# A fused attention and experts kernel: another order of the mixed stage, and the first transposition of the maxima moved into the attention

## The reference

```
x = x + attention0(group_norm(x))      # 6 heads of 16; relative position bias over rows and columns; no mask
t = x as tokens (1024, 96)
t = t + attention1(layer_norm(t))      # 6 heads of 16; causal mask
t = t + experts(layer_norm(t))         # 4 experts 96 -> 384 -> 96, softmax gate, the best 2 kept
```

## Time and profile before

| | |
|---|---|
| median of 3 executions | 2171.5 us (2166.65 to 2174.11) |
| the profiled execution | 2174.62 us, its span 2172.8 us, mean granted PE clock 0.929 of full speed |
| PE busy | 1873.2 us, 86% of the span |
| DVE busy | 1246.8 us, 57% |
| ACT busy | 1121.3 us, 52% |
| POOL busy | 145.3 us, 7% |

### The profile page before, as it was taken

One profiled execution on the slowest core, in us unless ns is written; L12 is line 12 of the kernel. 1 busy time (PEld: TensorE's weight loads), 2 busy tenths in 40 slices (PEclk: granted clock), 3 DMA queues, 4 the chain that ended last, 5 costly groups with the idle time before them and its releaser, 6 DMA issues.

```text
span 2172.8 us, 29007 instructions
## 1 busy us (share of the span) xinstructions
PE 1873.2 (86%) x9408; PEld 750.1 (35%) x9408; DVE 1246.8 (57%) x2508; ACT 1121.3 (52%) x1423; POOL 145.3 (7%) x69
## 2 busy tenths in 40 slices
PE   2696589988899888997899978998789988999858
PEld 1132233433334333343333433343333433334323
DVE  6671676456773567545665557645677357753631
ACT  3256245663466544673456734566346654556333
POOL 3000002000020001100020000200002000200000
PEclk7598599998999899999999989999899999999979
DMA  6326300632026300263004530064102630001200
GB/s 142 49 48 98 73 11 18 114 67 41 17 54 99 66 22 18 51 96 66 22 18 91 73 64 11 21 114 73 33 18 53 99 66 13 18 11 41 43 11 8
DMA packets 55742, 111.45 MB, mean 51 GB/s; under 512 B 17687, under 2 KB 18904, under 8 KB 54041
## 3 DMA queue, kind: packets, MB, share of 16 engines
q1 hardware_dynamic: 54040, 109.06, 26.9%
q10 hardware_dynamic: 1536, 0.30, 0.1%
HBM read 61.82 MB, written 34.60 MB: 44 GB/s over the span
## 4 chain that ended last, share of the span: by engine, by line
PE 67%; DVE 15%; issue 6%; ACT 5%; DMA 4%; SPq 1%; POOL 1%; DVEq 0%; ACTq 0%; POOLq 0%
PE psOM L646 15%; PE psS L592 12%; PE psT L621 8%; PE psT L622 7%; DVE mx L1280 6%; PE psT L756 6%; PE psS L770 5%; PE psT L624 3%; DVE mrow L1382 2%; PE psT L542 2%; DVE qb L1409 2%; DVE x L1391 1%; DMA qr<-negb 1%; PE psT L551 1%; PE psOM L567 1%
## 5 line engine op out<-in xcount | busy, mean ns | idle before, releaser
L1007 ACT ACTIVATE probs<-psT 128x1024 f32<-128x1024 f32 (+7 forms) x768 | 622.9, 838 | 540.2 <-PE psT L622 267.7
L1280 DVE TENSOR_REDUCE mx<-psS 128x1 f32<-128x512 f32 (+3 forms) x1152 | 704.4, 644 | 312.1 <-PE psS L592 233.6
L622 PE MATMUL psT<-qb,kb 97*128 97x512 f32 x768 | 417.2, 587 | 0.0
L646 PE MATMUL psOM<-probs,v 128*32 128x512 f32 (+3 forms) x2688 | 385.0, 558 | 13.0 <-ACT probs L1007 13.0
L592 PE MATMUL psS<-ka,qa 128*128 128x512 bf16 x768 | 300.9, 401 | 37.6 <-DVE mx L1280 18.8
L621 PE MATMUL psT<-qa,ka 128*128 128x512 bf16 x768 | 297.6, 388 | 16.4 <-DMA qb<-negr 8.1
L1409 DVE TENSOR_TENSOR qb<-psOM,qa 32x768 fp32r<-32x768 f32 x128 | 121.8, 952 | 139.7 <-ACT qa L1047 137.9
L756 PE MATMUL psT<-xf,w1s 97*128 97x512 f32 x384 | 198.4, 650 | 1.8 <-DVE mrow L1382 1.8
L770 PE MATMUL psS<-probs,w2s 128*96 128x512 f32 x384 | 189.8, 622 | 0.8 <-ACT att L1072 0.8
L624 PE MATMUL psT<-qr,kr 97*128 97x512 bf16 (+3 forms) x576 | 183.9, 346 | 3.5 <-DMA qr<-negb 1.3
L1064 ACT ACTIVATE probs<-psT 128x1024 f32<-128x1024 f32 x96 | 98.4, 1025 | 158.9 <-PE psT L756 158.3
(11 more groups left out here) (146 smaller groups left out, 1651.4 us busy)
## 6 DMA issues: line engine op xcount, KB each, us to landing
scr<-split SPq DMA_DIRECT2D x32, 576.0 KB, 4.5
scr<-qb SPq DMA_DIRECT2D x16, 768.0 KB, 6.6
qr<-scr SPq DMA_DIRECT2D x48, 192.0 KB, 6.8
au<-ot SPq DMA_DIRECT2D x192, 32.0 KB, 2.0
lb<-ot SPq DMA_DIRECT2D x192, 32.0 KB, 2.0
qr<-scr SPq DMA_DIRECT2D x48, 128.0 KB, 4.4
kr<-scr SPq DMA_DIRECT2D x48, 128.0 KB, 7.3
qa<-scr SPq DMA_DIRECT2D x32, 128.0 KB, 3.8
```

The costliest lines, as they stand in the source:

```text
L622: last = mm(o[:, a:b], kb[:, h, ks], qb[:, h, a:b], start=False, stop=True)
L646: last = mm(psO[j:j + 2 * HD, a - c * HALF:HALF], v[:, kt, 2 * p + hh, :], probs[:, (2 * kt + hh) % 4, a:(c + 1) * HALF], start=kt == 0, s ...
L1007: A(probs[:, n % 4, q0:T], psT[:, t_slot(ts, m), q0:T], ACT.Exp).then_inc(t_free, 1)
L1280: V.reduce_max(mx[layer][:, p % 2, (h % 2) * NT + t, kc:kc + 1], psS[:, s_bank(st, fill), 0:max_cols(layer, t, kc)], AX).then_inc(s_free, 1)
```

## The change

(In the first line "before" has H6 L6 behind d7.) The diff, cut to its core:

```diff
-"u11 m7 m8 m9 m10 d10 m11 m12 b2 m13 m14 d11 m15 b3 tmax")
+"u11 m7 m8 m9 m10 d10 m11 m12 b2 m13 m14 d11 m15 b3")
...
             def transpose_max(it, layer, p):
                 ms, n = att_m(layer, p)
-                pe.wait_ge(rowmax, upto("rowmax", it, ms, n + 1))
+                if layer == 1 and p == 0:
+                    pe.wait_ge(t_free, upto("t_free", it, ms, 0))
+                else:
+                    pe.wait_ge(rowmax, upto("rowmax", it, ms, p if layer else n + 1))
...
-                        if layer == 1 and p == 0:
-                            pe.wait_ge(y_free, upto("y_free", it, st, 0))
                         pe.wait_ge(o_free, upto("o_free", it, st, p))
...
                 if layer == 1:
+                    pe.wait_ge(y_free, upto("y_free", it, st, 0))
+                    transpose_max(it, 1, 0)
                     pe.wait_ge(l1_in, upto("l1_in", it, "attn1", 0))
                     for fill in range(LEAD):
                         max_scores(it, st, fill)
...
                     else:
-                        pe.wait_ge(negmax_in, upto("negmax_in", it, st, 16 * p))
+                        pe.wait_ge(negmax_in, upto("negmax_in", it, st, 16 * (p + 1)))
...
-            def first_rows(it, st):
-            def first_negated(it, st):
...
                 if layer == 1:
+                    neg_max(it, 1, 0)
                     exp_table()
```

More of the change, by code:

```diff
@@ L77, in seq @@
             for w in text.split()]
-MIX = seq("gate gates u0 u1 R0 d0 H0 L0 H1 L1 v0 u2 d1 v1 ln den R1 u3 d2 u4 H2 L2 u5 res H3 d3 nrm L3 u6 d4 d5 tr R2 H4 L4 q0 q1 lev V0 d6 V1 "
-          "u7 H5 L5 R3 u8 d7 H6 L6 H7 L7 u9 b0 d8 u10 b1 m0 m1 m2 m3 d9 m4 m5 m6 "
-          "u11 m7 m8 m9 m10 d10 m11 m12 b2 m13 m14 d11 m15 b3 tmax")
+MIX = seq("gate gates u0 u1 R0 d0 H0 L0 H1 L1 v0 u2 d1 v1 ln den R1 u3 H2 L2 d2 H3 u4 res d3 nrm L3 u5 d4 tr u6 R2 H4 L4 d5 q0 q1 V0 lev V1 "
+          "H5 L5 u7 d6 u8 R3 H6 L6 d7 H7 L7 u9 b0 d8 b1 u10 m0 m1 m2 m3 d9 m4 m5 m6 "
+          "u11 m7 m8 m9 m10 d10 m11 m12 b2 m13 m14 d11 m15 b3")
 def there(stage, kind):
@@ L112, in fills @@
 def fills(stage, kind):
-    return [x for x in steps(stage, kind) if x[0] in ("up", "max", "tmax", "res", "tr", "qk", "val", "val0")]
+    return [x for x in steps(stage, kind) if x[0] in ("up", "max", "res", "tr", "qk", "val", "val0")]
 def by_act(what):
-    return what[0] in ("up", "tr", "tmax", "val", "val0")
+    return what[0] in ("up", "tr", "val", "val0")
 _ATT = {"attn0": 1, "attn1": 1}
@@ L136 @@
     "t_full": {"p_qkv0": 4, "attn1": ATT_FILLS, "attn0": QKV_AT, "qkv0": 2,
-               "attn0b": ATT_FILLS - QKV_AT, "rel": 2, "a": NE * HJ, "next_mix": 7 + 2 * NT},
+               "attn0b": ATT_FILLS - QKV_AT, "rel": 2, "a": NE * HJ, "next_mix": 6 + 2 * NT},
     "s_full": {**{s: len(m) for s, m in MAX_STEPS.items()}, "norm": 4, "a": 2 * NE},
-    "m_full": {"attn1": PAIRS - 1, "lead": 1, "attn0": PAIRS - 1, "a": 1},
+    "m_full": {"attn1": PAIRS, "lead": 1, "attn0": PAIRS - 1, "a": 1},
     "gsum_full": _GN, "gsum_free": _GN,
@@ L151 @@
     "rowmax": {"attn1": PAIRS - 1, "lead": 1, "attn0": PAIRS - 1},
-    "negmax_in": {"attn1": 16 * (PAIRS - 1), "lead": 16, "attn0": 16 * (PAIRS - 1), "next_mix": 16},
+    "negmax_in": {"attn1": 16 * PAIRS, "lead": 16, "attn0": 16 * (PAIRS - 1)},
     "p_used": {s: ATT_FILLS for s in _ATT},
@@ L162 @@
     INCS[f"{_r}_free"] = dict(INCS[f"{_r}_full"])
-INCS["ta_free"] = {"p_qkv0": 2, "rel": 2, "a": NE * HJ, "next_mix": 4}
+INCS["ta_free"] = {"p_qkv0": 2, "rel": 2, "a": NE * HJ, "next_mix": 3}
 INCS["r_free"] = {"qkv0": 2}
@@ L217, in att_m @@
 def att_m(layer, p):
-    return ("attn1", p - 1) if layer else ("attn0", p - 1) if p else ("lead", 0)
+    return ("attn1", p) if layer else ("attn0", p - 1) if p else ("lead", 0)
 def next_layer0(it):
@@ L841, in mix @@
                         first_maxima(it, "mix", n)
-                    elif what == "tmax":
-                        first_rows(it, "mix")
-            def first_rows(it, st):
[L847 to L851, removed]
             def group_means(it, st):
@@ L966, in neg_max @@
                 act.wait_ge(m_full, upto("m_full", it, ms, n + 1))
-                act.wait_ge(negmax_in, upto("negmax_in", it, ms, 16 * max(p - 2, 0) if layer else 0))
+                act.wait_ge(negmax_in, upto("negmax_in", it, ms, 16 * max(p - 1, 0) if layer else 0))
                 A(negm[layer][:, p % 2, :], psM[0:2 * NT, 0:P], ACT.Copy, scale=-1.0).then_inc(m_free, 1)
@@ L1083, in mix @@
                         rel_high(it, "mix", n)
-                    elif what == "tmax":
-                        first_negated(it, "mix")
                     elif what == "up":
@@ L1283, in maxima @@
                         dve.wait_ge(s_free, upto("s_free", it, st, fill + 1))
-                        dve.wait_ge(m_full, upto("m_full", it, st, max(p - 1 - layer, 0)))
+                        dve.wait_ge(m_full, upto("m_full", it, st, max(p - 1, 0)))
                         V.tensor_tensor(mrow[:, p % 2, :], mx[layer][:, p % 2, :, 0], mx[layer][:, p % 2, :, 1],
```

## The result

The changed kernel has a median of 2159.99 us over 10 runs (2150.72 to 2170.08), the kernel before 2172.03 us over its 10 (2165.40 to 2178.93): ratio 0.9948, 95% interval 0.9925 to 0.9972. It is 0.5% faster, 12 us, where 28 had been forecast, and 2160 lies 2 us above the range. The runs of the changed kernel spread over 19 us, those before over 14. The profiled execution has a span of 2158.1 us, 14.7 less than before.

The account below looks back on a forecast made before the run. PE, busy 86% of the span, was taken as the bound. Terms -31.2 + 1.1 + 1.7 - 0.3 + 2.4 - 2.0 = -28.3 took 2174.6 to 2146.3 us, put as a median of 2143; range 2137 to 2157, chance 0.78.

Parts of the forecast that it names:

- mechanism of the gain: Full mixed stages: Gelus ahead of H5 and H6 in ACT's queue delay R3 and b0; R3's wait was 3.90 us.
- The replay of a full stage: Queues walked in the new order from u3: q0 1.15 us later, b0 5.35 us earlier.
- V0, V1, u7, d6, u8 until 994.7: Second half of a full stage: PE runs these until 994.7, so R3 finds L5 done and ends at 996.1.
- 5.2 us for each of six stages: Gain of the six full mixed stages, 31.2 us in all; bounds 3.5 and 6.0 per stage.
- The row that it went by: Earlier trace, 1010 to 1020: PE waits 1.4 and 1.3 us, is busy 75%, keeps clock 1.00; new waits cost nothing.
- The seventh stage: Mixed stage without bias: res waits 1.7 for att, tr 1.8, m0's levels come 2.5 later; +1.7 us.
- Slower, by the clock in the first half: Rival: waits before res, u5 and tr halve PE's clock, five products take 3.44 us each; +23, 2195 us; chance 0.05.
- The first stage: First mixed stage: no Gelu stands before H5, nothing won; V0 and V1 moved ahead delay R3, +1.1 us.
- The place of the transposition: Behind b3 at seven stage ends, now waiting for additions: +2.4 us at three straight ends, -2.0 at four loop branches.
- The DMA rival: R3's wait goes but m0 waits for its operands: 2.3 us won per stage, 2160 us; chance 0.13.

Follow-up runs that it names:

- H5 first: Kernel before the change with H5 and L5 put ahead of u7, and u8 ahead of R3, nothing else: 2125.82 us, ratio 0.9807.
- new first half: H5 first with the changed kernel's order from u3 to q0 in place of the old one: 2135.30 us, ratio 0.9821.
- the old order and the new place: Kernel before the change, mixed-stage order kept, first transposition moved into the attention behind the last addition: 2175.13 us, ratio 1.0021.
- b1 first: H5 first with b1 put ahead of u10, as in the changed kernel: 2126.99 us, ratio 0.9783.
- The kernel with d6 between: Changed kernel with d6 put back between V0 and V1 instead of between u7 and u8: 2148.21 us, ratio 0.9904.

## Why the prediction missed, step by step

**The direction and the mechanism of the gain were right.** u7's Gelu ahead of H5 makes R3 wait, and u8's Gelu, late through the half clock, holds H6: H5 first removes both and wins 45 us. Of the 28.3 forecast for the profiled execution 14.7 came. The six full stages gave 8.7 less than their term, the seventh cost 4.9 more, the start and first stage 1.3 more, and the ends of the stages 1.3 more; the attentions, at nothing in the sum, gave 2.5.

**The replay of a full stage was right where the clock held.** It put b0 5.35 earlier. The two warm stages have it 4.84 earlier. Of the waits, read in the third stage: u5 0.39 (said 0.6), tr 1.10 (1.3), R3 none, b1 0.37 (0.5); V0 waits 0.65 as in the kernel before.

**The step that failed** is the sentence that lets PE have "V0, V1, u7, d6, u8 until 994.7". I gave u7 and d6 1.72 each. It is the term "5.2 us for each of six stages": it measured 4.8 in the two warm stages, 3.2 on average in the other four, 22.5 in all instead of 31.2. I had priced half clock as a rival, but put it in the first half, at res, u5 and tr; there the clock held in all six stages, and with d6 between V0 and V1 it held behind them as well. What the prediction leaves out is that the new order takes the dense product d6 out from between two runs of short matmuls that each start with a wait. The row that it went by was read wrong in part, too: between 1010 and 1020 the timeline has one wait of 1.39 and others of 0.53 at most, not 1.4 and 1.3.

**The seventh stage** was sized +1.7 and measured +6.6. Res waited 1.53 for `att` as said (1.7), and tr 0.97 (1.8). The rest is clock: in this execution u1, res with d3, and u7 with d6 ran cold, each for part of a product. At res the rival *Slower, by the clock in the first half* did come true, in this stage alone:

```profile
1960.70:1964.20 3.50, 3.50 (x13) 2.37 (x13) 1.38 (x4) 0.89 (x1) 0.00 (x0) 0.51 0.01 2
```

The clock fell behind this wait of 1.53 in all four kernels with the new first half, and in none of the five with the old one, where u5 stands in front of res. Over the kernels the stage is 66.8 to 68.5 us long with the old first half and d6 in place, 70.6 with the new first half and d6 in place, and 72.9 to 73.9 with V0 and V1 together; so about 3 belong to the first half and 3 to the adjacency (with the old first half the adjacency alone cost 4.4).

**The first stage** was +1.1 by my steps. R3 starts at 242.84 instead of 240.73, +2.1. Some 1.4 of it is clock: the q products start within 0.1 us of where they did, but last 6.05 instead of 4.72, because PE was at half clock for 2.7 us longer in this execution. DVE's third level (L1415) takes 2.30 instead of 1.85, since it now overlaps POOL's third level for q longer (last section).

**The place of the transposition.** Between b3's start and `scores` the three straight ends measured +1.35, +0.98 and +0.58: 2.9 against 2.4. At two of them the LEAD products no longer cover the DMA of the negated maxima, which I had excluded. The changed kernel's timeline has one of the two:

```profile
1781.56 0.28 PE L605 MATMUL psOM<-cst,mrow 128*16 128x128 f32 x1 [2.51 <-DVE x L1372]
1785.95 0.61 PE L627 MATMUL psT<-qr,kr 97*128 97x512 bf16 x1 [0.25 <-DMA qr<-negb]
```

From the transposition to the first product that needs the DMA are 4.39 us, not the 2.9 at most that I had summed; the median of 1.7 to landing of these DMAs had hidden longer ones. The wait itself is only 0.25 and 0.16. Behind the third full stage, where the loop branches back, the same timeline shows the gap and, 4.36 later, the first `scores`:

```profile
1028.15 0.38 PE L605 MATMUL psOM<-cst,mrow 128*16 128x128 f32 x1 [4.72 <-issue]
1032.51 0.63 PE L627 MATMUL psT<-qr,kr 97*128 97x512 bf16 x1
```

The gap is 4.7 from b3's end, where I expected 3.97, so three of the four ends give -0.04, -0.09 and +0.20 and the fourth -1.27 (before, it was a long one): -1.2 against -2.0. With the old order and the new place the four lie at 8.2 to 9.1 from b3 to `scores`, 1.5 below the kernel before on average, where I had 0.5.

The trace does tell these gaps apart. One of the profile's DMA queues of kind "instruction", q8, moves blocks of 16 KB. Its row in the DMA view (queue: transfers, MB, share), for PE's gap behind the third full stage of the kernel before (1031.17:1035.13, 3.97 idle), behind its fifth (1546.08:1551.18, 5.10), behind the third of the changed kernel (1023.00:1028.15, 4.72), and of the old order with the new place (1024.46:1027.68, 3.22, ended by the additions):

```profile
q8 instruction: 1, 0.02, 1.6%
q8 instruction: 2, 0.03, 4.6%
q8 instruction: 2, 0.03, 4.9%
q8 instruction: 1, 0.02, 2.1%
```

So it is at all 36 such ends of the nine kernels. Where two blocks are on their way at once, the slower takes 1.8 to 2.6 us and PE's gap is 5.0 to 5.2 with the transposition in front of it and 4.7 to 4.8 without. Where they come singly, most take 0.9 to 1.4, and the gap is 3.5 to 4.0, or PE is back within 2.9 to 3.2 and waits for the additions. The changed kernel had two at once at all four ends, the kernel before at one. The Trainium skill (Runtime: NRT & Kernel Launch, Instruction fetch mechanics) says that a taken branch to a page that is not held stalls until a DMA has fetched it; these transfers agree with it. That they hold PE is inferred from the times, and why they overlap in one order and not in another stays open.

**The DMA rival** did not happen: no m0 of a full stage waited for its operands.

The parts add up: 2126 (H5 first) + 9.5 (new first half) + 1 (b1 first) + about 2 to 5 (place) gives 2139 to 2142. The kernel with d6 between, which differs from that only by lev behind V0, has 2148, and d6 moved behind brings it to the changed kernel's 2160. The place of lev was not tried alone, but the two traces show what it does: R3 waits 0.72 for L5 in each full stage where lev is behind V0, and not at all where it is in front (H5 first with the new first half), and b0 comes at 55.2 instead of 54.4 to 54.5. That is about 4.5 of the 6 to 9 us between sum and measurement.

## What to carry to other kernels

When an order written by hand is changed, look at what each product stands between. A dense product between two short ones that wait was worth more here than its cover of the waits, because it kept PE's clock; price a move by whether the stretch without it can go cold, and count the products behind it at half clock. In an in-order queue, the first question about a wait is what stands ahead of the releasing instruction: here one Gelu ahead of two small copies, with no product in front of the step that waited for them, cost 2% of the kernel, and the smallest edit that mends both beat the whole reordering.

## What the runs showed of the hardware

**Short waits between short matmuls went with a fall of the clock.** In the earlier trace rows a wait of 3.90 us came before the fall. In the changed kernel the waits are 0.65 and 0.58 with sixteen matmuls of 96 columns between and behind them, PE is busy 81% of that stretch (2.42 of 3 us), and the clock fell to half in four of six stages. With waits of 0.65, 0.58 and 0.33 it was busy 61% (2.44 of 4) and fell in all six. With d6 between, the stretch behind V0 was busy throughout (3.00 of 3) and the clock never fell there. Both edits that moved d6, one each way, moved the fall with it. But from 1010 to 1020 in the earlier trace rows PE was busy 75% and stayed at 1.00, so the busy share of a stretch does not tell it alone. The Trainium skill (TensorE: Matmul & The Clock Gate, What's actually happening) says that the slow state is the default and that activity lifts it. I had set that against a row in the prediction and gone by the row; the result agrees with the page, in the full stages at another place than I had feared, and in the seventh at res.

**The spread of the runs may come with it, in part.** The same stage takes 78.3 or 81.7 us from gate to b3 in one execution, and the changed kernel's runs lie between 2150.7 and 2170.1 us. Six stages that each win or lose 3.4 would make up 20 us. H5 first, whose profile shows the clock at 1.00 behind V0 and V1, has runs within 6.4 us. But H5 first with the new first half keeps the clock at V0 and V1 as well, and its six runs lie between 2127.3 and 2143.4, 16 apart; so this cannot be the only source of the spread. That the number of cold stages is what differs from run to run is argued from one profile of each kernel and was not shown run by run.

**An overlap of DVE and POOL was paid in full.** The third levels of q (POOL, 2.13 us) and k (DVE, L1434 before, L1415 after) run partly at the same time. Where the overlap was 0.77 us, DVE's took 1.85; where it was 1.22, in the order with V0 ahead of lev, 2.30. In all eight stages of both kernels the duration less the overlap is 1.08, as if DVE's operation stood still while POOL's ran.
